# Fused cross-attention and routed attention, one core: the head in another order, q, k and v weights prepared in three parts, o^T of the first group earlier on ScalarE

## The reference

```python
x = x + tanh(g_xattn) * cross_attention(ctx, layernorm(x), Wk, Wq, Wv)      # 77 keys for each sequence
h = layernorm(x)
logits = normalized(h) @ normalized(sim) - sigmoid(gates)                   # 16 experts
w = softmax(relu(logits) where > 0, with the top 2 where none is)
q, k, v = [sum over e of w[:, e] * (h @ proj[e]) for proj in (q_proj, k_proj, v_proj)]
o = softmax(q k^T / sqrt(128)) v                                            # within 128 tokens of a sequence
x = x + tanh(g_ffn) * sum over e of w[:, e] * (o @ o_proj[e])
```

## Time and profile before

| | |
|---|---|
| median of three runs | 800.28 us |
| the profiled execution | 799.99 us, its span 798.1 us |
| busy: PE, DVE, POOL, ACT | 776.1, 607.2, 483.0, 433.8 us |
| granted TensorE clock, mean | 0.987 of full speed |
| HBM over the span | 152 GB/s |

### The profile page before, as it was taken

One profiled execution on the slowest core, in us unless ns is written; L12 is line 12 of the kernel. 1 busy time (PEld: TensorE's weight loads), 2 busy tenths in 40 slices (PEclk: granted clock), 3 DMA queues, 4 the chain that ended last, 5 costly groups with the idle time before them and its releaser, 6 DMA issues.

```text
span 798.1 us, 13995 instructions
## 1 busy us (share of the span) xinstructions
PE 776.1 (97%) x3999; PEld 418.1 (52%) x3999; DVE 607.2 (76%) x2037; ACT 433.8 (54%) x1129; POOL 483.0 (61%) x703
## 2 busy tenths in 40 slices
PE   7489999999999999999999999999999999999998
PEld 6445545555455555545555554555555455544444
DVE  2977787878787787778777787877878786775648
ACT  5554645556555655655565565456556555544445
POOL 3276657674746757474675747567574755765534
PEclk9789999999999999999999999999999999999999
DMA  6564476563655636365563636546364654543100
GB/s 192 136 216 159 162 219 174 169 209 94 209 161 164 189 106 204 97 210 167 151 191 106 202 109 209 166 150 186 101 207 116 208 160 139 163 135 116 53 14 28
DMA packets 97476, 122.57 MB, mean 154 GB/s; under 512 B 14611, under 2 KB 69111, under 8 KB 97399
## 3 DMA queue, kind: packets, MB, share of 16 engines
q1 hardware_dynamic: 96679, 121.59, 49.6%
q10 hardware_dynamic: 720, 0.08, 0.1%
HBM read 97.32 MB, written 24.31 MB: 152 GB/s over the span
## 4 chain that ended last, share of the span: by engine, by line
PE 88%; DVE 5%; DMA 2%; POOL 1%; ACT 1%; issue 1%; SPq 0%; DVEq 0%; ACTq 0%; POOLq 0%
PE acc_q L1380 20%; PE acc_k L1380 20%; PE acc_v L1380 20%; PE y L1409 9%; PE oT_p L1409 9%; PE m L1489 2%; PE m L1553 2%; DVE x_all L1175 1%; PE oT_p L1641 1%; PE m L1480 1%; PE m L1539 1%; DMA stage<-in_L_ffn_q_proj_dram 1%; PE m L1469 1%; POOL zq L658 1%; PE m L1529 1%
## 5 line engine op out<-in xcount | busy, mean ns | idle before, releaser
L658 POOL TENSOR_TENSOR zq<-zq_full,zq 128x512 f16<-128x512 f32 x256 | 297.8, 1170 | 222.4 <-ACT zq L743 222.2
L743 ACT ACTIVATE zq<-zq_full 128x512 f16<-128x512 f32 x256 | 160.1, 636 | 224.1 <-DVE zq_full L1145 224.0
L1175 DVE SCALAR_TENSOR_TENSOR x_all<-y,w_out,x_all 128x128 f32<-128x128 f32 x356 | 122.2, 343 | 96.1 <-issue 69.5
L1380 PE MATMUL acc_q<-zq,w_hi 128*128 128x512 f16 x510 | 193.3, 379 | 1.0 <-POOL zq L658 1.0
L1380 PE MATMUL acc_k<-zq,w_hi 128*128 128x512 f16 x510 | 193.2, 379 | 0.0
L1380 PE MATMUL acc_v<-zq,w_hi 128*128 128x512 f16 x510 | 193.2, 379 | 0.0
L1145 DVE TENSOR_TENSOR zq_full<-wq_bc,x2T_p 128x512 f32<-128x512 f32 x256 | 167.8, 668 | 2.5 <-DMA wq_bc<-w_rows 1.7
L1175 DVE SCALAR_TENSOR_TENSOR x_all<-oT_p,w_out,x_all 128x128 f32<-128x128 f32 x356 | 121.5, 341 | 0.0
L673 POOL TENSOR_TENSOR x_all<-stage,x_all 128x128 f32<-128x128 f32 x240 | 100.4, 456 | 19.8 <-DVE x_all L1175 13.3
L1380 PE MATMUL acc_q<-zq,w_lo 128*128 128x512 f16 x255 | 96.6, 379 | 0.0
L1380 PE MATMUL acc_v<-zq,w_lo 128*128 128x512 f16 x255 | 96.6, 379 | 0.0
(11 more groups left out here) (253 smaller groups left out, 1091.4 us busy)
## 6 DMA issues: line engine op xcount, KB each, us to landing
wq_bc<-w_rows SPq DMA_DIRECT2D x128, 512.0 KB, 4.5
blk_rows<-stage SPq DMA_DIRECT2D x26, 256.0 KB, 2.7
stage<-blk_rows SPq DMA_DIRECT2D x104, 64.0 KB, 2.0
blk_rows<-v_blk SPq DMA_DIRECT2D x15, 256.0 KB, 2.0
v_mix<-blk_rows SPq DMA_DIRECT2D x60, 64.0 KB, 2.9
blk_rows<-pc_blk SPq DMA_DIRECT2D x15, 256.0 KB, 4.1
pcT<-blk_rows SPq DMA_DIRECT2D x60, 64.0 KB, 2.0
out_dram<-x_all SPq DMA_DIRECT2D x15, 256.0 KB, 6.7
```

The lines of the kernel that those rows point to most:

```text
L658: nc.gpsimd.tensor_tensor(zq[:, 1, e % Z_SLOTS, :], zq_full[:, e % F_SLOTS, :], zq[:, 0, e % Z_SLOTS, :], ALU.subtract).then_inc(zq_lo_poo ...
L743: nc.scalar.activation(zq[:, 0, e % Z_SLOTS, :], zq_full[:, e % F_SLOTS, :], ACT.Copy).then_inc(zq_hi_done, 1)
L1175: nc.vector.scalar_tensor_tensor(out=rows(x_all, g, b0 + b), in0=bank[:, tok(j)], scalar=w_out[:, g % 2, e, b0 + b:b0 + b + 1], in1=rows(x ...
L1380: last = nc.tensor.matmul(acc[m][:], w[:, m, s, :], zq[:, half, s % Z_SLOTS, :], start=(s == 0 and n == 0), stop=(s == E - 1 and n == 2))
```

## The change

It leaves the computation as it is and moves instructions in the head and in the first two passes.

- SP: q's weights are loaded ahead of the contexts of groups 1 to 3, and x of group 1 (`load_x(1)`) ahead of v's weights. The first pair of broadcast rows comes in two DMAs of 256 KB with a semaphore each.
- The high and low halves of the q, k and v weights are made in three parts: experts 0 to 3, 4 to 7, 8 to 15. The first part of all three and the second of q are ready ahead of the first product's input; the second parts of k and v come on DVE around step 0 of pass 0, and the last parts in steps 2, 3 and 4 (on ACT in steps 1 and 2).
- DVE's head: `first_stats(1)` ahead of v's `weight_max`, the gate of group 0 ahead of `weight_scales`, `x1_add(1)` ahead of `zq_scale(0, 0)`, `first_stats(2)` in step 1 of pass 0.
- ACT: `x2_norm(1)` at the end of the head, ahead of `zq_high(0, 4)` instead of behind `zq_high(0, 5)`.
- POOL: `first_rstd(2)` behind `zq_low(0, 6)` instead of ahead of `zq_low(0, 4)`.
- PE: the attention product of group 0 ahead of the contexts of groups 1 to 3, the gate's products ahead of `gather_max`, and 22 `keep_busy` in seven places instead of 8 in one; the first expert's high products first.
- `O^T`: in pass 1, ACT's copy of o^T (`oT_high(0)`) stands ahead of the `zq_high` of step 8 instead of behind it. The other passes are unchanged in this.
- `HIGH_AT` and `LOW_AT` (o's weights) are one step later each.

```diff
--- before.py
+++ after.py
@@ -38,6 +38,8 @@
...
 PRE = 3
+PARTS = ((0, 4), (4, 8), (8, 16))
 GATE_STEPS = 12
...
@@ -410,6 +413,11 @@
         def vx_bank(g):
             return (acc[V], oT_p, acc[K])[g - 1] if 1 <= g <= PRE else m0
+        def split_part(t, m, part):
+            experts = slice(*PARTS[part]) if m < O else slice(0, E)
+            return t[:, m, experts].rearrange("p e h -> p (e h)")
         def ctx_slot(g):
...
@@ -495,17 +503,21 @@
             def head():
                 sp.wait_ge(kq_in, 16 * 2)
+                load_weights(Q, q_proj)
                 sp.dma_start(zq_full[0:S, 0:PRE].rearrange("p k (b c) -> p (k b) c", b=G),
                              c_v[:, G:G * (PRE + 1), :]).then_inc(ctx_pre_in, 16)
-                load_weights(Q, q_proj)
                 load_weights(K, k_proj)
+                load_x(1)
                 load_weights(V, v_proj)
-                load_x(1)
                 load_weights(O, o_proj)
...
                 weight_rows(0)
-                for j in range(W_SLOTS):
+                for e, done in enumerate((wq_first_in, wq_in[0])):
+                    src = w_rows[0:1, G * e:G * (e + 1), :].rearrange("a r n -> (a r n)")
+                    sp.dma_start(wq_bc[:, 0, e], src.partition_broadcast(P)).then_inc(done, 16)
+                for j in range(1, W_SLOTS):
                     spread_q(0, j)
...
-                first_rstd(2)
             def body(i):
...
@@ -695,6 +706,8 @@
...
                         zq_low(g, e)
+                    if i == 0 and s == 2:
+                        first_rstd(2)
                     if s == 1 and i < 2:
...
@@ -732,9 +745,9 @@
...
                 nc.scalar.activation(exp_0[:], tanh_f[:], ACT.Exp)
-            def weight_high(m):
+            def weight_high(m, part=0):
                 act.wait_ge(scales_done, 1 if m < O else 2)
-                nc.scalar.activation(w_hi[:, m], stage[:, m], ACT.Copy,
+                nc.scalar.activation(split_part(w_hi, m, part), split_part(stage, m, part), ACT.Copy,
                                      scale=w_up[:, m:m + 1]).then_inc(hi_done[m], 1)
...
@@ -876,6 +889,11 @@
...
                                          px_mix[:].rearrange("p i b n -> p b i n"), ACT.Copy).then_inc(pxT_sb, 1)
+            def oT_high(g):
+                wait(act, oT_ps, g + 1)
+                wait(act, y_ps, PAIRS_Y * (g - 1))
+                nc.scalar.activation(oT[:, g % 2, 0, :], oT_p[:], ACT.Copy).then_inc(oT_hi_done, 1)
             def head():
...
@@ -887,28 +905,32 @@
...
                 vx_out(0)
-                ctxT_out(1)
                 pxT_out(0)
-                ctxT_out(2)
-                ctxT_out(3)
-                kxT_out(1)
-                vx_out(1)
-                for g in range(2, PRE + 1):
+                for g in range(1, PRE + 1):
+                    ctxT_out(g)
+                for g in range(1, PRE):
                     kxT_out(g)
...
                 x2_norm(0)
+                kxT_out(PRE)
                 x2T_out(0)
-                weight_high(Q)
                 x_norm(1)
+                vx_out(PRE)
                 gate_exps(0)
...
                 x2T_move(0)
+                x_exps(1)
+                weight_high(Q)
                 weight_high(K)
-                x_exps(1)
                 pxT_out(1)
                 weight_high(V)
-                for e in range(LEAD):
+                weight_high(Q, 1)
+                weight_high(K, 1)
+                zq_high(0, 0)
+                weight_high(V, 1)
+                for e in range(1, LEAD):
                     zq_high(0, e)
+                x2_norm(1)
             def body(i):
...
@@ -926,8 +948,15 @@
...
                         y_scale(gd, 7, banks=(1,))
+                    if i == 1 and s == Y_FIRST:
+                        oT_high(0)
                     for g, e in zq_at(i, s):
                         zq_high(g, e)
+                    if i == 0 and s == 1:
+                        weight_high(Q, 2)
+                        weight_high(K, 2)
+                    if i == 0 and s == 2:
+                        weight_high(V, 2)
                     if s == 6 and has(gd) and i < NG:
...
@@ -937,7 +966,7 @@
...
                                              ACT.Copy).then_inc(v_tok_sb, 1)
-                    if s == 1 and i < 2:
+                    if s == 1 and i == 1:
                         x2_norm(g2)
...
@@ -969,10 +998,8 @@
...
                         kxT_out(g1)
-                    if s == Y_FIRST and has(gc):
-                        wait(act, oT_ps, gc + 1)
-                        wait(act, y_ps, PAIRS_Y * (gc - 1))
-                        nc.scalar.activation(oT[:, gc % 2, 0, :], oT_p[:], ACT.Copy).then_inc(oT_hi_done, 1)
+                    if s == Y_FIRST and i > 1 and has(gc):
+                        oT_high(gc)
                     if s == 10 - sooner(i) and has(g1):
...
@@ -1063,12 +1090,11 @@
...
                     nc.vector.tensor_scalar(out_scale[:], out_scale[:], tanh_f[:], None, ALU.mult).then_inc(scales_done, 1)
-            def weight_low(m):
-                dve.wait_ge(hi_done[m], 1)
+            def weight_low(m, part=0):
+                dve.wait_ge(hi_done[m], part + 1)
                 nc.vector.scalar_tensor_tensor(
-                    out=w_lo[:, m].rearrange("p e h -> p (e h)"), in0=stage[:, m].rearrange("p e h -> p (e h)"),
-                    scalar=w_up[:, m:m + 1], in1=w_hi[:, m].rearrange("p e h -> p (e h)"),
-                    op0=ALU.mult, op1=ALU.subtract).then_inc(lo_done[m], 1)
+                    out=split_part(w_lo, m, part), in0=split_part(stage, m, part), scalar=w_up[:, m:m + 1],
+                    in1=split_part(w_hi, m, part), op0=ALU.mult, op1=ALU.subtract).then_inc(lo_done[m], 1)
             def blocks_transposed(dst, src, done):
...
@@ -1138,7 +1164,9 @@
...
                     wait(dve, ctxT_ps, e + 2)
-                if e % 2 == 0:
+                if (g, e) == (0, 0):
+                    dve.wait_ge(wq_first_in, 16)
+                elif e % 2 == 0 or (g, e) == (0, 1):
                     j = e // 2
...
@@ -1235,33 +1263,40 @@
...
                 weight_max(K)
+                first_stats(1)
                 setup_gate()
+                x2_norm_inverse(0)
                 weight_max(V)
+                gate_logits(0)
                 share_largest(0)
-                first_stats(1)
-                weight_scales(0)
-                x2_norm_inverse(0)
-                gate_logits(0)
                 gate_mask(0)
                 gate_softmax(0)
+                x_max(1)
+                weight_scales(0)
                 weight_low(Q)
-                x_max(1)
                 weight_low(K)
                 x_sum(1)
+                weight_low(V)
+                x1_add(1)
+                weight_low(Q, 1)
                 zq_scale(0, 0)
                 zq_scale(0, 1)
-                weight_low(V)
+                second_stats(1)
                 zq_scale(0, 2)
-                x1_add(1)
-                second_stats(1)
                 zq_scale(0, 3)
-                first_stats(2)
+                weight_low(K, 1)
             def body(i):
...
                         zq_scale(g, e)
+                    if i == 0 and s == 0:
+                        weight_low(V, 1)
+                    if i == 0 and s == 1:
+                        first_stats(2)
+                    if i == 0 and s in (2, 3, 4):
+                        weight_low((Q, K, V)[s - 2], 2)
                     if s == 11 - sooner(i) and P_HEAD <= g1 < NG:
...
@@ -1374,6 +1409,10 @@
...
                 for m in (Q, K, V):
+                    for part, (first, _) in enumerate(PARTS):
+                        if (i, s) == (0, first):
+                            pe.wait_ge(hi_done[m], part + 1)
+                            pe.wait_ge(lo_done[m], part + 1)
                     if s == 0:
...
@@ -1394,6 +1433,7 @@
...
                     nc.tensor.matmul(acc[m][:], w_hi[:, m, 0, :], zq[:, 0, 0, :], start=True, stop=False)
+                for m in (Q, K, V):
                     pe.wait_ge(lo_done[m], 1)
...
@@ -1572,29 +1612,33 @@
...
                 vx_product(0)
+                px_transpose(0)
+                att_product(0)
                 for g in range(1, PRE + 1):
                     ctx_transpose(g)
-                px_transpose(0)
-                kx_product(1)
-                att_product(0)
-                vx_product(1)
-                for g in range(2, PRE + 1):
+                for g in range(1, PRE + 1):
                     kx_product(g)
...
                 pe.wait_ge(kxT_sb, 3)
-                keep_busy(8)
+                keep_busy(1)
                 x2_transpose(0)
-                pe.wait_ge(vx_sb, PRE + 1)
-                gather_max(0, acc[V])
+                keep_busy(1)
                 pe.wait_ge(prep_dve, 4)
...
                     small_product(-1, 4, b)
-                spread_max(0, acc[K])
+                keep_busy(2)
```

(12 more changed lines are left out.)

## The result

The changed kernel took 806.35 us in the median of seven runs (804.15 to 806.96), beside 800.39 us of the kernel before on the same chip: ratio 1.0066, 95% interval 1.0055 to 1.0076. The medians are 6.0 us apart. The result lies 0.95 us above the range of the prediction (798.3 to 805.4), 3.05 us above its number. The profiled execution took 804.67 us (span 802.9, mean granted clock 0.989), 4.68 us more than that of before.

What follows compares the result with a forecast made beforehand. PE, busy 776.1 of 798.1 us, was taken to bound the kernel. Expert 5's delay +3.2, clock +1.3 and o^T −1.2 made +3.3 us on 799.99: 803.3 us, range 798.3 to 805.4.

Steps and rivals of the forecast that it cites:

- The head: Start of the kernel up to PE's first product: it starts at about 39.6 us, 3.6 us earlier than before.
- so I take full clock there: Head: with 22 fillers PE idles no more than some 1.5 us at a time, so its clock stays full.
- the clock drops in the head: Rival, head: gaps between fillers put PE's clock at 0.50, products take 2 us longer, total 805.3 us; chance 0.09.
- Expert 4: Pass 0 on PE: expert 4 starts at about 49.7 us, about 4.7 us earlier than before.
- Term 1: Expert 5, pass 0: POOL steps and `w_lo` exclude each other, group 1's gate product comes later; +3.2 us, bounds 0 to +4.4.
- Term 2: After PE's idle stretch of 51.6 to 60.1 us: clock at 0.50 costs +1.3 us, bounds 0 and 1.9.
- Term 3: Pass 1: ACT's earlier copy of o^T removes PE's wait before the first product with it; −1.2 us, bounds −1.25 and −0.8.
- The sum: Whole kernel: +3.2 + 1.3 − 1.2 = +3.3 us on the profiled 799.99 us, giving 803.3 us.
- Small steps don't wait: Rival, POOL in pass 0: four-channel steps are not held up by `w_lo`, gate product stays put, 800.1 us; chance 0.18.
- The lead is kept: Rival, pass 0: PE keeps expert 4's 4.7 us, total 794.1 us, or 796.4 with half; chance 0.12 for under 798.3.
- Late loads: Rival, head: x of group 1 or k's weights land 1 us later, first product only 2.6 us earlier, 804.3 us; chance 0.08.

Runs made afterwards that it cites:

- e3_rstd: The changed kernel with only POOL's `first_rstd(2)` put back ahead of the low half of expert 4 of group 0: 804.02 us, ratio 1.0042.
- e6_lows: The changed kernel with the last `w_lo` parts of q, k and v all behind DVE's `zq_scale` of expert 8: 804.8 us, ratio 1.0066.
- e7_rstd_x2n: The changed kernel with POOL's `first_rstd(2)` back ahead of expert 4's low half and ACT's `x2_norm(1)` behind expert 5's high half: 797.91 us, ratio 0.9965.
- e2_busy: The changed kernel with filler matmuls in PE's two waits of pass 0, 11 before o's weight maxima, 22 before group 1's gate product: 804.4 us, ratio 1.0046.
- e4_oT: The kernel before with only ACT's copy of o^T in pass 1 moved ahead of the `zq_high` of step 8: 799.53 us, ratio 0.999.
- e9_more: The changed kernel with both calls back, last `w_lo` parts behind expert 8's `zq_scale`, ten head fillers, plus 21 more at 22 to 40 us: 798.57 us.
- e8_all: The changed kernel with `first_rstd(2)` and `x2_norm(1)` back, last `w_lo` parts behind expert 8's `zq_scale`, ten head fillers: 796.71 us, ratio 0.9958.

## Why the prediction was wrong, by its own steps

- **The head.** First product at 39.6 us: 39.82 in the first trace, right. In the two further traces it was 41.30 and 41.06. The step "so I take full clock there" held in none of the three. In the first trace the clock was at 0.50 from 35.34 to 38.75 us, which fell on the last fillers (16 matmuls in 3.14 us), and PE still waited 0.41 us for ACT behind them, so it cost nothing: that the first product came at its number is in part luck. The rival "the clock drops in the head" (805.3 us, priced at 2 us) is the mechanism of the other two, at 1.2 to 1.5. Its place was another than I had named: in one trace the contexts of groups 1 to 3; in the other group 0's own first products (the gate product came 0.9 us later, at 26.14 instead of 25.24) and the products from 26.7 us on (`px_transpose(1)` 1.4 us later, at 34.57 instead of 33.14). DVE, which waits for both kinds, shows it: 1.78 us of waiting for the gate product in the one, 2.14 instead of 1.25 us for group 0's attention product in the other. The gate product of group 0 is queued behind the contexts; before, DVE reached the gate's arithmetic only at 29.62 us, with these products done at 27.7. So the change made the head depend on PE's clock more than it did.
- **Expert 4** at 49.7: 49.44 us, right.
- **Term 1, +3.2 us**: +2.64. The mechanism was right, and the runs show it twice, by the root put back (e3_rstd, −2.86 us) and by the long steps that went where the `w_lo` went (e6_lows). `x2_norm(1)`, which the chain has too, weighs as much: with both calls back 5.9 of the 6.0 us that B had grown by are gone (e7_rstd_x2n). The size was off by 0.6: I let `second_norm(1)` start at 51.9, behind q's last part. It started at 50.52 and only its first step was held up, for 0.9 us. The Trainium skill, page "SBUF — State Buffer", section "Who interferes with whom", states that whoever issues first keeps the shared port pair and the other blocks fully; by that rule the steps of 128x4 had to wait as well, and the trace agrees: they took 0.56 to 1.22 us instead of 0.20 to 0.23.
- **Term 2, +1.3 us: the step that failed.** I took the length of the half clock behind a wait from the one row before, 2.6 us, with an upper bound of 3.8 us of work, 1.9 us lost, which no row shows. It was 6.5 us of PE's full work at 0.50, and 3.14 us lost (C: 7.67 against 4.53); 3.10 in the second trace and 1.66 in the third. e2_busy took exactly this term away and changed nothing else there. The forecast and its upper bound leaned on one stretch of one trace, which bounds nothing.
- **Term 3, −1.2 us**: −1.06 in the trace, −1.27 with that part alone (e4_oT). Right.
- **The sum.** With the measured sizes: +2.64 + 3.14 − 1.06 = +4.7 on 799.99, the profiled 804.67. The median is 1.7 us above it, which is the size of the head's later first product, and of the seven first runs four lay at 806.4 to 807.0. That those four had it is not shown; they have no trace themselves. More time at half clock alone isn't it, since their mean granted clocks are 0.983 to 0.994, three of them above the 0.987 to 0.989 of the three faster runs. Where the half clock falls would fit, and so would a wait as in pass 1 of e9_more. So Term 2 accounts for the profiled execution, and the last 1.7 us of the median stay open.
- **The other rivals.** "Small steps don't wait" is out by the rows. "The lead is kept" (794.1 to 796.4) is out for this order, but its condition, the root of group 2 ahead of the last parts, is what e7_rstd_x2n and e8_all restore (with `x2_norm(1)` put back as well), and their medians of 797.9 and 796.7 us are near what it gave. "Late loads" didn't happen: the first product shows it.

## What to carry to other kernels

An earlier start is worth what the next shared engine can pass on: here 3.4 us at the first product turned into 2.6 us of loss twenty microseconds later. The split of the weights was not what cost this: with two calls back at their places (POOL's root of the next group ahead of the parts, ACT's norm behind the inputs of the experts) the same split left B at 13.86 us, 0.15 us more than before. Before you put a call that others wait for behind work of a neighbouring group, look at what will run beside it; put the two-input DVE steps where POOL computes nothing small that others wait for. Price a clock that fell from several stretches and leave the bound wide, since its cost in one and the same place was 1.66 and 3.1 us; in these traces it was about half of the time for which PE had work at 0.50. And where a change puts PE on the path of a stretch with little work, count on a wider spread of the runs, not only on the profiled one.

## What the runs showed of the hardware

The granted clock at 0.50 (the 1.2 GHz level) fell on different stretches in three executions of the same kernel: 11.45 to 14.86 and 35.34 to 38.75 us; 16.32 to 23.15 us; 9.66 to 16.48, 26.73 to 30.14 and 36.97 to 40.38 us. Behind PE's wait in pass 0 it fell in all three. A root of 128x4 on POOL took up to 1.92 us beside three `w_lo` in a row (e6_lows), a multiplication of 128x4 2.25 us under one of 128x2048 (the changed kernel), and in the rows shown none of POOL's steps was longer beside `weight_max` (1.04 us for a root, 0.23 us for the steps of e8_all).
